# An attention and mixture-of-experts layer: every expert gets slots for all sorted tokens, so that two of three batches' rows are sent during attention

## The reference, cut to what matters

```python
# x: (4, 1024, 128); every layernorm without scale unless named
x = x + layernorm(attention(layernorm(x)))          # 16 heads of 64, softmax over all 1024 keys
x = x + layernorm(experts(layernorm(x)))

def experts(x):                                      # E = 8 experts, hidden size F = 256
    probs = softmax(x @ router)
    weights, chosen = top_k(probs, 2)                # two experts for each token
    w = softmax(weights)
    return sum over the two chosen experts e of w_e * ((silu(x @ gate[e]) * (x @ up[e])) @ down[e])
```

## Time and profile before

| what | us |
|---|---|
| median of 3 runs | 1510.72 (1507.89 to 1512.13) |
| the profiled execution's own time | 1509.74 |
| its span, first to last instruction | 1506.8 |
| PE busy | 1399.6 (93%) |
| POOL busy | 1231.8 (82%) |
| DVE busy | 1172.8 (78%) |
| ACT busy | 1058.2 (70%) |

### The profile page before, as it was taken

The page is one execution under the profiler, slowest core; times in us unless marked ns, Lnnn a source line. Parts: engine busy times, 40 slices in busy tenths (PEclk is TensorE's granted clock), DMA queues, the critical chain, the costliest instruction groups (busy, mean ns, idle before and its releaser), DMA issues.

```text
span 1506.8 us, 45151 instructions
## 1 busy us (share of the span) xinstructions
PE 1399.6 (93%) x17865; PEld 930.3 (62%) x17865; DVE 1172.8 (78%) x2688; ACT 1058.2 (70%) x2048; POOL 1231.8 (82%) x742
## 2 busy tenths in 40 slices
PE   4899999999999999999999999999999888969995
PEld 1366665666666665666665656666666555659994
DVE  7788887777788788878788788777887888845576
ACT  2777777777777877777788777777877665724344
POOL 5588999888988988989889888899789878825374
PEclk7899999999999999999999999999999998979998
DMA  6433333422232223222333223233232242133222
GB/s 177 116 112 111 113 108 89 110 75 79 61 90 81 72 79 100 79 79 79 88 83 86 79 78 88 76 82 83 73 86 71 58 161 68 45 119 97 68 58 73
DMA packets 101487, 132.86 MB, mean 88 GB/s; under 512 B 16672, under 2 KB 51232, under 8 KB 100896
## 3 DMA queue, kind: packets, MB, share of 16 engines
q1 hardware_dynamic: 98208, 123.70, 29.7%
q0 software_dynamic: 3072, 6.30, 1.5%
HBM read 20.49 MB, written 14.94 MB: 24 GB/s over the span
## 4 chain that ended last, share of the span: by engine, by line
PE 36%; POOL 10%; DVE 3%; issue 2%; ACT 2%; DMA 1%; POOLq 0%; SPq 0%; DVEq 0%; ACTq 0%
PE psum L1013 5%; PE psum L806 5%; PE psum L911 5%; PE psum L909 5%; POOL slots_in L1974 4%; PE psum L1039 3%; PE psum L930 3%; PE psum L932 3%; PE psum L934 3%; POOL probs_lo L1925 2%; PE psum L790 1%; PE psum L831 1%; PE psum L823 1%; POOL oacc L1934 1%; POOL rot L1909 1%
## 5 line engine op out<-in xcount | busy, mean ns | idle before, releaser
L1186 ACT ACTIVATE probs<-psum 128x512 f32<-128x512 f32 x1024 | 614.9, 604 | 197.8 <-PE psum L911 196.9
L1925 POOL TENSOR_TENSOR probs_lo<-probs 128x1024 f16<-128x1024 f32 x301 | 618.8, 2067 | 108.4 <-ACT probs L1186 107.3
L1473 DVE CUSTOM_DVE_ANT_0 scan_out<-psum,ahead 128x512 f16<-128x512 f32 x512 | 349.0, 685 | 198.3 <-PE psum L806 189.7
L930 PE MATMUL psum<-cv,probs 128*128 128x66 f16 x4096 | 476.8, 193 | 12.6 <-POOL probs_lo L1925 12.1
L932 PE MATMUL psum<-cv,probs 128*128 128x64 f16 x4096 | 476.4, 194 | 0.0
L934 PE MATMUL psum<-cv,probs_lo 128*128 128x66 f16 x4096 | 475.1, 192 | 0.0
L932 PEld LDWEIGHTS psum<-cv,probs 128*128 128x128 bf16 x4096 | 380.7, 97 | 110.8 <-issue 3.1
L930 PEld LDWEIGHTS psum<-cv,probs 128*128 128x128 bf16 x4096 | 385.8, 97 | 73.5 <-POOL probs_lo L1925 13.2
L909 PE MATMUL psum<-q_both,k_twice 128*128 128x512 f16 x1024 | 388.9, 380 | 2.9 <-ACT probs L1186 2.9
L911 PE MATMUL psum<-q_max,k_ones 65*128 65x512 f16 x1024 | 391.3, 382 | 0.0
L934 PEld LDWEIGHTS psum<-cv,probs_lo 128*128 128x128 f16 x4096 | 380.3, 98 | 0.0
(11 more groups left out here) (219 smaller groups left out, 1908.9 us busy)
## 6 DMA issues: line engine op xcount, KB each, us to landing
t_swapped<-t_sin SPq DMA_DIRECT2D x248, 128.0 KB, 2.0
k_twice<-qk_hi SPq DMA_DIRECT2D x128, 128.0 KB
q_lone<-qk_hi SPq DMA_DIRECT2D x64, 128.0 KB, 2.3
q_both<-qk_hi SPq DMA_DIRECT2D x64, 128.0 KB
q_both<-qk_lo SPq DMA_DIRECT2D x64, 128.0 KB
q_max<-qk_hi SPq DMA_DIRECT2D x64, 128.0 KB, 2.3
k_ones<-qk_lo SPq DMA_DIRECT2D x64, 128.0 KB, 2.4
z_unit<-slots_in SPq DMA_DIRECT2D x31, 128.0 KB, 2.3
```

What stands on the lines that cost most here:

```text
L930: pe.matmul(acc, high[:, q * P:(q + 1) * P, 1], v[:, 0:VLO], start=opens, stop=False, skip_group_check=True)
L1186: act.activation(probs[s % 4][:, i, :], score_ps[tile % SCORE_BANKS], ACT.Exp, scale=SCALE).then_inc(probs_done, 1)
L1473: dve.tensor_tensor_reduce(scan_out[m % 2][:], bank[BANK_OF["base", n, m]], ahead[m % 2][:], 1.0, LOWEST, ALU.add, ALU.max, max_all[a][:, ...
L1925: pool.tensor_tensor(probs_lo[s % 4][:].rearrange("p a n -> p (a n)"), p, p.bitcast(BF16).rearrange("p (n two) -> p n two", two=2)[:, :, 1 ...
```

## The change

Each expert now has its own range of 3072 slots (`MOST_UNITS * UNIT`), enough for every token of three batches. So a token's slot is its expert's number times 3072 plus its rank among the tokens so far, which is known as soon as its own batch is ranked. `take_ranks` writes it at once, with one more DVE instruction. There is one DRAM tensor, `slots`, of 26368 rows of 512 bytes (7936 before), for the rows in and the results out; seven units at its end serve those of the 31 that no expert fills. Clearing it takes 26 transfers, up to four in each of stretches 1 to 7, spread over SP's program. `place` no longer makes slots; it makes `row_of`, the first row of each unit, and SP reads that into registers, four at a time, for each load and store.

The sends of batch 0 stand in stretches 14 to 21 (2, 2, none, 3, 2, 2, 2, 3), of batch 1 in 22 to 27 (2, 3, 3, 3, 3, 2), of batch 2 in 30 and 31 (8 each). A stretch with two has them at steps 1 and 9, with three at 1, 6 and 11, with eight at each odd step. Each send waits for the exponentials up to its own step. `LATE_DVE_STEPS` now gives DVE 6, 8 and 12 steps in stretches 29, 30, 31. The fetches also wait, each for a certain dense unit.

```diff
+SLOTS = E * MOST_UNITS * UNIT
+ALL_SLOTS = SLOTS + (SORTED - CHOICES * MOST_UNITS) * UNIT
...
-LATE_DVE_STEPS = {GROUPS - 3: (2, 4, 6, 8, 10, 13, 15), GROUPS - 2: (0, 1, 2, 3, 5, 6, 7, 8, 9, 11, 12, 13, 14, 15),
-                  GROUPS - 1: tuple(range(STEPS))}
+LATE_DVE_STEPS = {GROUPS - 2: (1, 3, 5, 7, 9, 11, 13, 15), GROUPS - 1: (0, 1, 2, 4, 5, 6, 8, 9, 10, 12, 13, 14)}
...
-SEND_AT = ([(LAST - 2, s) for s in (11, 12, 13, 14, 15, 15)]
...
+SEND_AT = [(g, s) for stretches in (((14, 2), (15, 2), (17, 3), (18, 2), (19, 2), (20, 2), (21, 3)),
+                                    ((22, 2), (23, 3), (24, 3), (25, 3), (26, 3), (27, 2)), ((30, 8), (31, 8)))
+           for g, many in stretches for s in range(1, STEPS, STEPS // many) if s // (STEPS // many) < many]
+FIRST_GATHER = 2
...
-            def clear_slots(at, n):
-                width = n * 2 * D // P
-                sp.dma_start(slots_in[at:at + n, :].rearrange("(p r) d -> p (r d)", p=P),
-                             oacc[1][:].bitcast(F16)[:, 0:width]).then_inc(cleared, 16)
+            def clear_slots(g, i):
+                if not 0 < g < PAIRS or 4 * (g - 1) + i >= len(to_clear):
+                    return
+                at, n = to_clear[4 * (g - 1) + i]
+                sp.dma_start(slots[at:at + n, :].rearrange("(p r) d -> p (r d)", p=P),
+                             oacc[1][:, 0:n * D // P]).then_inc(cleared, 16)
+
+            rows_from = [sp.alloc_register(f"row_from{i}") for i in range(IDS_AT_ONCE)]
+            rows_to = [sp.alloc_register(f"row_to{i}") for i in range(IDS_AT_ONCE)]
+
+            def first_row(unit, regs):
+
+                if unit % IDS_AT_ONCE == 0:
+                    sp.wait_ge(placed, 1)
+                    sp.load(regs, row_of[0:1, unit:unit + IDS_AT_ONCE])
+                return sp.snap(regs[unit % IDS_AT_ONCE], min_val=0, max_val=ALL_SLOTS - UNIT)
 
             def load_unit(unit):
+                first = first_row(unit, rows_from)
                 if unit >= SLOTS_IN:
                     sp.wait_ge(unit_turned, unit - SLOTS_IN + 1)
-                sp.dma_start(z_unit[unit % SLOTS_IN][:], unit_rows(slots_in, unit)).then_inc(unit_in[unit % SLOTS_IN], 16)
+                sp.dma_start(z_unit[unit % SLOTS_IN][:].bitcast(F32), unit_rows(first)).then_inc(unit_in[unit % SLOTS_IN], 16)
...
-                dve.tensor_reduce(ranks[:, n], rank_parts[:], AX, ALU.add).then_inc(ranked, 1)
+                step(dve.tensor_reduce(ranks[:, n], rank_parts[:], AX, ALU.add), 2)
+                dve.scalar_tensor_tensor(out=slot_of[:, n], in0=top_at[:, :, 0:CHOICES].rearrange("p t k -> p k t"),
+                                         scalar=float(MOST_UNITS * UNIT), in1=ranks[:, n], op0=ALU.mult,
+                                         op1=ALU.add).then_inc(ranked, 1)
...
-                for (n, t, k), at in zip(SENT, SEND_AT):
-                    if at != (g, s):
-                        continue
+                here = [sent_row for sent_row, at in zip(SENT, SEND_AT) if at == (g, s)]
+                for i, (n, t, k) in enumerate(here):
                     if (t, k) == (0, 0):
-                        pool.wait_ge(placed, 1)
+                        pool.wait_ge(ranked, n + 1)
                         pool.wait_ge(z_lo_done, CHUNKS * (n + 1))
+                    if 2 * s + i:
+                        pool.wait_ge(probs_done, g * KEY_TILES + 2 * s + i)
                     send(n, t, k)
...
             for made, (j, t, k) in enumerate(gathers):
+                beside = FIRST_GATHER + made // 2
+                if made % 2 == 0:
+                    pool.wait_ge(fuse_done, SORTED + beside + 1)
+                else:
+                    pool.wait_ge(added, beside - DOWN_LAG + 1)
                 fetch(j, t, k)
```

More of the change, by code:

```diff
@@ L474, in final_place @@
             return final_bank(j)[:, at * P:(at + 1) * P]
-        to_clear = [(at, min(clear_rows, SORTED * UNIT - at)) for at in range(0, SORTED * UNIT, clear_rows)]
+        to_clear = [(at, min(clear_rows, ALL_SLOTS - at)) for at in range(0, ALL_SLOTS, clear_rows)]
         cleared, clear_set = sem("cleared"), sem("clear_set")
@@ L548, in in_dram, with unit_rows @@
             return t[bass.ds(b, 1)].rearrange("b (t p) d -> p (b t) d", p=P)
-        def unit_rows(rows, unit):
-            return rows[unit * UNIT:(unit + 1) * UNIT, :].rearrange("(i p) d -> p i d", p=P)
+        def unit_rows(first):
+            return slots[bass.ds(first, UNIT), :].rearrange("(i p) d -> p i d", p=P)
         def dense(unit):
@@ L686, in _ @@
                         sp.wait_ge(clear_set, 1)
-                    for piece in to_clear[2 * (r - 1):2 * r]:
-                        clear_slots(*piece)
+                    clear_slots(r, 0)
                 if epoch and r == 3:
@@ L708, in _ @@
                     swap_rows(g + 2, 1)
+                clear_slots(g, 1)
                 put_both(g + 1, 1)
@@ L716, in _ @@
                     put_lone(g + 2)
+                clear_slots(g, 3)
                 if g < PAIRS - 2:
@@ L1623, in take_ranks, with step @@
             def take_ranks(n):
+                def step(ins, k):
+                    ins.then_inc(rank_steps, 1)
+                    dve.wait_ge(rank_steps, 2 * n + k)
                 dve.wait_ge(rank_ready, n + 1)
@@ L1656, in place @@
-                step(dve.tensor_tensor(base_parts[:, 0:rows], own, slot_base[:].unsqueeze(1).to_broadcast([P, rows, E]), ALU.mult), 6)
-                dve.tensor_reduce(expert_of[:], past[:], AX, ALU.add)
-                step(dve.tensor_reduce(base_sum[:, 0:rows], base_parts[:, 0:rows], AX, ALU.add), 7)
-                step(dve.tensor_scalar(column_of[:], expert_of[:], float(E - 1), float(F), ALU.min,
-                                       ALU.mult), 8)
-                to = slot_of[:, 0:EARLY].rearrange("p b k t -> p (b k t)")
@@ L1662, in place @@
-                step(dve.tensor_tensor(to, base_sum[:, 0:rows], ranks[:, 0:EARLY].rearrange("p b k t -> p (b k t)"),
-                                       ALU.add), 9)
+                step(dve.tensor_tensor(past[:], unit_at[:].unsqueeze(2).to_broadcast([1, COLUMNS, E]),
+                                       unit_ends[0:1, :].unsqueeze(1).to_broadcast([1, COLUMNS, E]), ALU.is_ge), 4)
+                dve.tensor_tensor(jumps[:], past[:], unused[:].unsqueeze(1).to_broadcast([1, COLUMNS, E]), ALU.mult)
@@ L1664, in place @@
+                step(dve.tensor_reduce(expert_of[:], past[:], AX, ALU.add), 5)
+                step(dve.tensor_reduce(jump[:], jumps[:], AX, ALU.add), 6)
+                dve.tensor_scalar(column_of[:], expert_of[:], float(E - 1), float(F), ALU.min, ALU.mult)
+                step(dve.tensor_tensor(row_of[:], jump[:], steps_of[0:1, :], ALU.add), 7)
                 standing()
```

38 lines of the change are left out of this document (16 added, 22 removed).

## The result

The changed kernel takes 1578.6 us (median of 4 runs, 1578.11 to 1580.93) where the kernel before takes 1510.84 on the same chip: ratio 1.045, 95% interval 1.043 to 1.046. The prediction said 1501 and 1490 to 1512. The profiled execution took 1579.02, its span is 1577.0, so 70.2 us more than the span of before.

The account below looks back on a forecast made before the run. PE was taken to set the pace in most stretches, with POOL a few us to spare. Terms 12.9 - 3.5 - 9.3 - 12.0 + 2 = -9.9 took the span from 1506.8 to 1496.9, so 1501 us; range 1490 to 1512.

Parts of the forecast that it names:

- In the other direction I see no loss: Sends beside DVE: sends cost POOL 2.0 us each, but a DVE remainder took its 1.22 us while sends ran.
- the early sends' term: Stretches 14 to 27: 32 early sends at 2.0 us nearly fit POOL's 61.0 us idle; +12.9 us, bounds 4 and 22.
- The rule of the Trainium skill: DVE and GpSimd ports: by it a send stays near 1.26 us among DVE's remainders, early sends costing about 4, not 13.
- POOL becomes the bound: Rival, stretches 14 to 27: without POOL idle time DVE's instructions wait and scans hold PE's banks; 1518 to 1530, chance 0.12.
- the sends did not hide: Answers the rival that the early sends hide altogether in POOL's slack: cost 4 us, 1488 to 1494, chance 0.2.
- the swaps were not the matter: Answers the rival that clearing transfers delay the swaps in SP's queue: 9 us, 1508, chance 0.1.
- the seam closed: Answers the rival that POOL stays late in stretch 31: seam gives 6 instead of 12, stretch 30 gives 5; 1511, chance 0.12.
- Stretch 30: Attention's stretch 30: PE and POOL both nearly full, 37 us instead of 46.32; -9.3 us, bounds -5 and -11.
- stretch 29: Attention's stretch 29: loses its sends, gains a POOL remainder, keeps 3.8 us behind `place`; -3.5 us, bounds 0 and 6.5.
- Behind the start of stretch 31: Seam to the expert phase: last send earlier, PE starts sooner on the first unit; -12.0 us, bounds -9 and -13.5.
- just fit: Stretch 31 stays at 26.83 us: POOL's four remainders, eight sends and two sums fit; otherwise late by up to 2.
- Up to stretch 14: Clearing: 18 more transfers of 512 KB in SP's queue, 0.1 us each; +2 us, bounds 0 and 9.

Follow-up runs that it names:

- x2: Changed kernel with the send and DVE-remainder tables of the kernel before, plus 32 POOL sums of two SBUF tensors at the early places: 1530.6 us.
- x3: Changed kernel with the send and DVE-remainder tables of the kernel before, plus 32 POOL memsets at the early places: 1522.6 us.
- x11: Kernel before the change, with a one-element memset and a wait for it behind each of stretch 29's six sends: 1509.3 us, ratio to before 0.9992.
- x4: Changed kernel with a one-element memset and a wait for it behind each of the 32 early sends: 1506.8 us, ratio to before 0.9976.
- x1: Changed kernel with the tables of sends and DVE remainders of the kernel before, so sends late again: 1516.4 us, ratio to before 1.0035.
- x5: x4 with all 16 remainders of stretch 31 on DVE again, in place of 12: 1503.8 us, ratio to before 0.9956.
- x6: Changed kernel with x4's memset and wait ahead of each early send instead of behind it: 1581.8 us, ratio to before 1.0476.
- x7: Changed kernel with all 32 early sends at step 6, no pause added: 1587.4 us, ratio to before 1.0515.
- x8: Changed kernel with all 32 early sends at step 11, no pause added: 1591.5 us.
- x9: x5 with the memset behind each early send but no wait for it: 1602.6 us, on a chip where the kernel before took 1568.4.

## Why the prediction was wrong

**The step that failed** is "In the other direction I see no loss". I looked for what a send costs POOL, and from one remainder of 1.22 us during late sends concluded that DVE loses nothing. That row stands in stretch 31, where POOL has no remainders and waits behind nearly every send. The sends around it, in the timeline of POOL before:

```profile
1293.74 1.98 POOL L1974 DMA_INDIRECT slots_in<-z_rows,slot_of  x1 [0.30 <-issue]
1296.03 1.43 POOL L1974 DMA_INDIRECT slots_in<-z_rows,slot_of  x1 [0.30 <-issue]
```

The remainder starts 0.31 us before the end of the first, and behind it POOL stands still for 0.30. The early sends stand in rows of POOL work without a gap, and the same group had the right case in it: `z_rows` of 4.90 us, behind a send at 1233.31. I read that as a loss to POOL's dense computing. x2 and x3 show that dense computing alone does not do it, and x11 that a pause behind the sends takes the 4.90 away. I had even named the instructions behind that send; what I did not do was to ask whether such rows without a send hold DVE as long. The 103 remainders in such rows in the trace of before are not held so. What followed from the step: the early sends' term was put at 12.9 us and measured 91.7, of which 74.6 go with the hold.

**The early sends' own time** was right in size: with the hold removed (x4) stretches 14 to 27 take 17.1 us more, against 12.9 and a high bound of 22, and that includes 0.16 us for each breath (0.18 less 0.02), 5 us of POOL's time in all. How much longer a send gets beside DVE was read rightly too: in the changed kernel the sends that start while DVE is in an instruction with two SBUF inputs take 1.78 us in the median and 1.99 at most, the others 0.98 in the median. By stretch: 24 +3.0 (I said 3.6), 25 +3.1 (2.7), 21 and 23 together +2.0 (2.6), 19 and 27 together +3.0 (4.0), the others +6.0 (0; there the cover that I named is only part of a cover).

**The rule of the Trainium skill** was weighed for the wrong side. "SBUF — State Buffer", section "Who interferes with whom", says that DVE and GpSimd take their shared ports as an exclusive lock for a whole instruction, and that the loser blocks fully. Rows without a send agree: a wait of one instruction, then the turn (3.15 us at most). Behind a send the trace disagrees: the wait goes over five and more instructions, up to 10.98 us.

**The rivals.** "POOL becomes the bound" gave the right sign and the right place (DVE's remainders wait, the scans behind them hold up PE's banks), and 1518 to 1530 (the 1518 does not come out of its own terms: half the sends at 1.3 is 21 us and gives 1509, or 1515 with half of the 12.9 for the rest). But its mechanism was wrong: POOL still waits 170 us for exponentials, and it was put as a matter of how much the sends cost. A held instruction costs about 6 us here ((91.7 - 17.1) / 12), and it is the number of them that counts. The other three fell: the sends did not hide, the swaps were not the matter, the seam closed.

**The late terms.** Stretch 30 gave 11.4 (I said 9.3, bound 11), but 9.4 in the six of nine traces in which it takes 36.9; stretch 29 gave 2.3 (3.5), and 1.4 to 4.3 over the nine. Behind the start of stretch 31 it is 11.2 for 12.0, but by two errors that cancel: the stretch itself grew by 4.0 where I said "just fit" (my own terms, 7.4 + 16.0 + two sums below 1.9 each, come to as much as 27.2 against 26.83), and the rest (the seam and the experts) gave 15.2. The waits for the first unit in the changed kernel:

```profile
PE psum L1023 <- DMA z_unit<-slots: 1.2, 1, 1.2
```

PE waits 1.2 us where it waited 14.7; I had said some 3. The register load took 0.76 us from the landing of the last send to the issue of the load in x1's chain (1.0 in my sum). x5 shows that part of stretch 31's growth comes from POOL's four remainders: 3.5 us of x4's 5.6. Up to stretch 14 the kernel is 3.4 us longer and x1 3.5, for 2 in my sum; the nine traces have 2.8 to 6.6, within the bounds.

## What to carry to other kernels

A new instruction on a shared resource has a price on its own engine and one on its neighbour's: look in the trace for the neighbour's longest single instruction of each kind (mean and maximum), not only at a typical one, and compare rows that differ in one thing. When a DMA is issued from POOL in the middle of POOL's computing, put a pause behind it (a memset of one element and a wait for it), or issue it where POOL waits anyway. If POOL's neighbour DVE has an instruction with two SBUF inputs on the path, check its duration around every such issue.

## What the runs showed of the hardware that I had not expected

- A DVE instruction with two SBUF inputs that starts during or behind a send in a row of POOL instructions without a gap ends only after the row: 4.05 to 11.51 us for `probs_lo`, `k_diff`, `z_rows`, `pr` and `gap`, in 57 cases over the changed kernel, x6, x7, x8 and x9. In the same rows scans that read PSUM take their 0.69.
- A pause of 0.09 us behind the send is enough; the same pause ahead of it (x6), or the memset without a pause (x9), does nothing.
- Not every such start is held, and the traces show which are. Take, behind or during each send with more POOL work in its row, the first of these DVE instructions that starts; the traces of before, changed, x1 to x3 and x6 to x9 have 150. The 37 that start 0.67 us or more before the end of the send take 0.69 to 1.25 us. Of the 113 that start from 0.61 us before that end on, 111 end at most 1.09 us behind the end of POOL's row, whether that comes 0.13 or 10.96 us after their start; so many short ones are held too, and the row merely ends soon. In the trace of before they are 8. The two exceptions (x6 at 661.64, x9 at 945.63) end 1.1 us behind a POOL instruction in mid-row, and are not explained.
- Where a remainder started that early and was still in progress when the send ended, as beside the send at 638.32 of the changed kernel (remainder at 638.64, 1.21 us), the later ones of the row went on as rows without a send do. Being in progress at that end is not what spares one: the remainder at 1088.22 above was, and took 10.47. Why the start decides was not tried by itself.
